# Attention output by features through transfers instead of TensorE transposes

## What is computed

```
q, k, v = split_heads(modulate(ln(x)) @ W_qkv)       # cross: k, v from the context
a = softmax(q @ k.T / sqrt(16))                      # per head
out = (a @ v).reshape(B, tokens, 256)
x = x + gate * (out @ W_out + b_out)
```

## Time and profile before

| | us |
|---|---|
| median of 3 runs (2801.97 to 2818.2) | 2812.86 |
| the profiled execution | 2808.65 |
| its span | 2806.5 |
| TensorE matmul busy | 2694.6 |
| VectorE busy | 1821.8 |
| ScalarE busy | 1442.5 |
| GpSimd busy | 291.4 |

### The profile page before, as it was taken

One profiled execution on the slowest core, in us unless ns is written; L12 is line 12 of the kernel. 1 busy time (PEld: TensorE's weight loads), 2 busy tenths in 40 slices (PEclk: granted clock), 3 DMA queues, 4 the chain that ended last, 5 costly groups with the idle time before them and its releaser, 6 DMA issues.

```text
span 2806.5 us, 57501 instructions
## 1 busy us (share of the span) xinstructions
PE 2694.6 (96%) x21118; PEld 1992.1 (71%) x21118; DVE 1821.8 (65%) x4675; ACT 1442.5 (51%) x2293; POOL 291.4 (10%) x346
## 2 busy tenths in 40 slices
PE   7989999999999999999999999999999999999998
PEld 5656777777776766666777777777776776776777
DVE  4576656755765367675667676676777667676652
ACT  1344554455454556454555555555555555556553
POOL 0000000000001111110111111111000000000000
PEclk9899999999999999998999999999999999999999
DMA  6434243333234365643433333333243332422410
GB/s 201 143 107 126 89 125 103 94 99 128 89 90 126 93 202 168 194 148 105 128 122 116 113 121 109 120 110 121 89 145 111 104 111 87 133 90 81 134 60 17
DMA packets 295964, 326.28 MB, mean 116 GB/s; under 512 B 85386, under 2 KB 186858, under 8 KB 295372
## 3 DMA queue, kind: packets, MB, share of 16 engines
q1 hardware_dynamic: 263244, 275.52, 32.3%
q10 hardware_dynamic: 32256, 47.07, 4.6%
q0 software_dynamic: 192, 0.01, 0.0%
HBM read 203.42 MB, written 118.31 MB: 115 GB/s over the span
## 4 chain that ended last, share of the span: by engine, by line
PE 75%; DVE 11%; DMA 5%; issue 3%; ACT 3%; SPq 2%; POOL 0%; ACTq 0%; DVEq 0%; POOLq 0%
PE gen L1329 12%; PE gen L1320 10%; PE gen L1195 10%; PE gen L1278 9%; PE gen L1161 9%; DVE row_max L1652 6%; PE score L1253 4%; PE score L1208 3%; PE score L1237 3%; PE gen L1289 3%; PE score L1223 3%; PE score L1259 3%; PE gen L1170 2%; PE gen L1300 2%; DMA max_scratch<-maxT 1%
## 5 line engine op out<-in xcount | busy, mean ns | idle before, releaser
L1652 DVE TENSOR_REDUCE row_max<-score 128x4 f32<-128x1024 f32 (+1 forms) x640 | 650.0, 1046 | 123.2 <-PE score L1237 104.4
L1469 ACT ACTIVATE probs<-score 128x1024 f32<-128x1024 f32 (+1 forms) x576 | 567.9, 1023 | 259.6 <-PE score L1253 151.8
L1320 PE MATMUL gen<-xnT,w_w1M 128*128 128x256 f32 x1536 | 361.9, 386 | 1.6 <-ACT xnT L1411 1.6
L1329 PE MATMUL gen<-w_w2M,hT 128*128 128x256 f32 x1536 | 352.3, 383 | 4.5 <-ACT hT L1495 4.4
L1505 POOL TENSOR_TENSOR rstd<-var_eps,minus_half 128x2 f32<-128x2 f32 x160 | 112.0, 700 | 2170.4 <-DVE var_eps L1548 2158.0
L1329 PEld LDWEIGHTS gen<-w_w2M,hT 128*128 128x128 f32 x1536 | 287.0, 191 | 51.5 <-issue 11.8
L1320 PEld LDWEIGHTS gen<-xnT,w_w1M 128*128 128x128 f32 x1536 | 283.7, 191 | 49.4 <-ACT xnT L1411 2.5
L1411 ACT ACTIVATE xnT<-gen,mod_all 128x256 f32<-128x256 f32 x288 | 146.9, 564 | 146.5 <-PE gen L1170 144.3
L1476 ACT COPY oT<-gen 128x512 f32<-128x512 f32 x224 | 131.8, 588 | 163.5 <-PE gen L1278 163.4
L1495 ACT ACTIVATE hT<-gen,b_b 128x256 f32<-128x256 f32 x384 | 157.7, 472 | 112.8 <-PE gen L1320 111.8
L1223 PE MATMUL score<-k_self,q_stack 64*128 64x256 f32 x1536 | 190.4, 340 | 21.3 <-DVE row_max L1652 17.5
(11 more groups left out here) (162 smaller groups left out, 4219.6 us busy)
## 6 DMA issues: line engine op xcount, KB each, us to landing
q_stack<-parts_scratch SPq DMA_DIRECT2D x336, 256.0 KB
parts_scratch<-parts ACTq DMA_DIRECT2D x160, 256.0 KB, 2.6
parts_scratch<-parts SPq DMA_DIRECT2D x160, 256.0 KB, 3.0
k_self<-parts_scratch SPq DMA_DIRECT2D x144, 256.0 KB, 3.7
k_cross<-parts_scratch SPq DMA_DIRECT2D x192, 78.0 KB, 2.5
x_scratch<-x SPq DMA_DIRECT2D x48, 256.0 KB, 3.4
x_in<-x_scratch SPq DMA_DIRECT2D x48, 256.0 KB, 2.8
gate<-gates_scratch SPq DMA_DIRECT2D x80, 128.0 KB, 3.4
```

The source lines that it names most:

```text
L1320: mm = pe.matmul(buf[:, i * S:i * S + S], w["M"]["w1"][:, fc, col:col + P], xnT[s][:, fc, :], start=fc == 0, stop=fc == FC - 1)
L1329: mm = pe.matmul(buf[:, 0:D], hT[:, j, c * P:c * P + P], w["M"]["w2"][:, j, :], start=j == 0, stop=j == FFC - 1)
L1469: act.activation(probs[st.probs][0:keys, :, :], score[st.fill.buf][0:keys, :, :].rearrange("p a (r q) -> p (a r) q", r=2), ACT.Exp, bias=k ...
L1652: dve.tensor_reduce(dst, src, AX_X, ALU.max).then_inc(max_done[b], 1)
```

## The change

The transposes `oX` and `atT` go, and so does `ae`. The stationary operand of `W` is now 32 columns for each head: in `v_self` and `v_cross` two heads lie interleaved (feature d of the one at 1 + 2d, of the other at 2 + 2d, ones at both ends), and the head of a matmul decides at which column its window of 32 starts. So per 32 partitions the heads of the first group have sums in row 0 and features in the odd rows, those of the second group sums in row 31 and features in the even rows; the rows between hold products with the neighbour's columns that nobody reads. `pv` copies the bank to `oT` and the second group also straight into `atT`; then SyncE places the sums of four heads twice (`sg`, two transfers of 4 rows) and the first group's 64 odd rows over the odd rows of `atT` (`sh`). The `oT` buffer comes free when all three have landed. When both halves' sums are there `dv` (`invert`) turns them, takes reciprocals and spreads them over features with a second transpose; `nm` (`divide`) multiplies all of `atT` by them, and `out` may run. The rows of the output weights are loaded in the new order of features by two transfers in place of one. V's copy or bias addition becomes two instructions in place of one.

In the planner, steps of `TRANSFERS` cost 1.4 times their measured time (`MARGIN`), the age of a job counts 16 instead of 12 (`AGE`), and some costs have other values.

```diff
-VC = HD + 1
+VC = 2 * HD + 2
...
+MARGIN, AGE, STAY = 1.4, 16, 4
...
-            "ST": 0.34 + 0.43 * mask if whole else 0.3, "ex": 0.92, "W": 0.99 if whole else 0.56, "pv": 0.48,
-            "oX": 0.44, "dv": 0.63, "atT": 0.22 if whole else 0.44, "ae": 0.26 if whole else 0.48, "out": 1.73,
+            "ST": 0.34 + 0.43 * mask if whole else 0.3, "ex": 0.92, "W": 0.99 if whole else 0.56, "pv": 0.85,
+            "sg": 3.4, "sh": 2.6, "dv": 1.35, "nm": 0.63, "out": 1.73,
...
-        self.before, self.cost = [], cost(blk, name, j)
+        self.before, self.cost = [], cost(blk, name, j) * (MARGIN if name in TRANSFERS else 1.0)
...
-    if name == "oX":
+    if name in ("sg", "sh"):
         gives += ("back",)
...
             pv = add("pv", h, "act", sums, sums[0])
-            oX = add("oX", h, "pe", [pv])
-            divided.append(add("dv", h, "dve", [oX], oX))
...
+            gathered.append(add("sg", h, "sp", [pv]))
+            placed.append(add("sh", h, "sp", [pv]))
+        scaled = add("nm", 0, "dve", [add("dv", 0, "dve", gathered)] + placed)
+        out = add("out", 0, "pe", [scaled])
...
-                st = min(can, key=lambda st: (12 * st.job - st.rank - 4 * (eng == "pe" and TILES.get(st.name, "whole") == self.tiles), 0))
+                st = min(can, key=lambda st: (AGE * st.job - st.rank - STAY * (eng == "pe" and TILES.get(st.name, "whole") == self.tiles), 0))
...
+                def place_sums(st):
+                    s, h, buf = st.slot, st.j, of(st, "pv", st.j).buf
+                    sp.wait_ge(*moved(of(st, "pv", h).fill))
+                    sp.dma_start(sums[s][2 * h + 1:P:VW, 0, :], oT[buf][0:P:VW, 0, :]).then_inc(sums_placed[buf], 16)
+                    sp.dma_start(sums[s][2 * h:P:VW, 0, :], oT[buf][VW - 1:P:VW, 1, :]).then_inc(sums_placed[buf], 16)
+
+                def place_heads(st):
+                    s, h, buf = st.slot, st.j, of(st, "pv", st.j).buf
+                    sp.wait_ge(*moved(of(st, "pv", h).fill))
+                    sp.dma_start(atT[s][1:P:2, h, :], oT[buf][1:P:2, 0, :]).then_inc(heads_placed[buf], 16)
...
-                            mm = pe.matmul(pv[VW * i:VW * i + VC, within, :], value, e, start=kc == 0,
+                            mm = pe.matmul(pv[VW * i:VW * i + VW, within, :], value, e, start=kc == 0,
...
                 def project_out(st):
                     s, blk = st.slot, st.blk
-                    for h in range(HALVES if blk.whole else 1):
-                        pe.wait_ge(*moved(of(st, "atT", h)))
+                    pe.wait_ge(divided, of(st, "nm").nth_all)
...
-                        act.copy(oT[st.buf][:, :, :], pv).then_inc(gen_moved[st.fill.buf], 1)
...
+                        act.copy(oT[st.buf][:, :, :], pv)
+                        act.copy(atT[s][:, j, :], pv[:, 1, :]).then_inc(gen_moved[st.fill.buf], 1)
...
+                def invert(st):
+
+                    s = st.slot
+                    for h in range(HALVES):
+                        dve.wait_ge(*sums_in(of(st, "sg", h)))
+                    link(dve.transpose(sums[s][:, 1, :], sums[s][:, 0, :]))
...
+                    for h in range(HALVES):
+                        dve.wait_ge(*heads_in(of(st, "sh", h)))
+                    dve.tensor_tensor(atT[s][:, :, :], atT[s][:, :, :], inverse[s][:, :, :], ALU.mult).then_inc(divided, 1)
```

More of the change, by code:

```diff
@@ L217, in gives_needed @@
 def gives_needed(blk, ring):
-    return {"hid": TC, "parts": 2, "queries": blk.uses, "gates": TC if blk.kind == "mlp" else 1}.get(ring, 1)
+    return {"hid": TC, "parts": 2, "back": 2, "queries": blk.uses, "gates": TC if blk.kind == "mlp" else 1}.get(ring, 1)
 class Program:
@@ L499, in run @@
                 st.nth_way = seen[st.name, st.slot, "way", st.j, st.blk.whole or st.j == 0]
-def chunks_of(blk, h):
-    return [h] if blk.whole else list(range(FC))
 def column(n):
@@ L839, in dit_stack @@
         xnT = per_slot("xnT", [P, FC, S])
-        at, delta, atT = xhat, xhat, xnT
+        sums, inverse, delta, atT = xhat, xhat, xhat, xnT
         ctx_in = [sb(f"ctx_in{i}", [CTX, D]) for i in range(CTX_IN)]
@@ L869, in dit_stack @@
         rows_ready = [slot_sems(f"rows_ready{h}_") for h in range(HALVES)]
+        sums_placed, heads_placed = ([sem(f"{n}{i}") for i in range(BACKS)] for n in ("sums_placed", "heads_placed"))
+        divided = sem("divided")
         biased = sem("biased")
@@ L1436, in _ @@
                             wait_own(st)
-                            src, out = gen[st.fill.buf][:, :].rearrange("p (c h d) -> p c h d", c=TC, h=H), v_self[own(st)][:, :, :, 0:HD]
+                            src, out = gen[st.fill.buf][:, :], v_self[own(st)][:, :, :, :].rearrange("p c n v -> p (c n) v")
                         else:
                             wait_cross(st)
-                            src, out = gen[st.fill.buf][0:CTX, 0:D].rearrange("p (h d) -> p h d", h=H), v_cross[cross_of(st)][:, :, 0:HD]
-                        act.copy(out, src).then_inc(gen_moved[st.fill.buf], 1)
+                            src, out = gen[st.fill.buf][0:CTX, 0:D], v_cross[cross_of(st)][:, :, :]
+                        for e in range(PER_HALF):
+                            ins = act.copy(interleaved(out, e), by_group(src, e))
+                        ins.then_inc(gen_moved[st.fill.buf], 1)
                     elif st.name == "ph":
@@ L1631, in values @@
                             dve.wait_ge(weighed, before.nth_all)
-                        dve.tensor_tensor(v_cross[cross_of(st)][:, :, 0:HD], src, vb, ALU.add).then_inc(gen_moved[st.fill.buf], 1)
+                        src, vb = gen[st.fill.buf][0:CTX, 0:D], bias_tile(st.blk, "ckv")[0:CTX, :]
+                        for e in range(PER_HALF):
+                            ins = dve.tensor_tensor(interleaved(v_cross[cross_of(st)][:, :, :], e), by_group(src, e), by_group(vb, e), ALU.add)
+                        ins.then_inc(gen_moved[st.fill.buf], 1)
                         return
@@ L1636, in values @@
                         dve.wait_ge(weighed, before.nth_all)
-                    vb = bias_tile(st.blk, "qkv")[:, :].rearrange("p (h d) -> p h d", d=HD)
+                    vb = bias_tile(st.blk, "qkv")[:, :]
                     for c in range(TC):
-                        src = gen[st.fill.buf][:, c * D:c * D + D].rearrange("p (h d) -> p h d", d=HD)
-                        ins = dve.tensor_tensor(v_self[own(st)][:, c, :, 0:HD], src, vb, ALU.add)
+                        src = gen[st.fill.buf][:, c * D:c * D + D]
+                        for e in range(PER_HALF):
+                            ins = dve.tensor_tensor(interleaved(v_self[own(st)][:, c, :, :], e), by_group(src, e), by_group(vb, e), ALU.add)
                     ins.then_inc(gen_moved[st.fill.buf], 1)
```

111 lines of the change are left out of this document (49 added, 62 removed).

## The result

| | before | after |
|---|---|---|
| median, us (range of 7 runs each) | 2812.86 (2801.97 to 2818.2) | 2783.06 (2773.33 to 2796.76) |
| ratio to before, 95% interval | | 0.9904 [0.9883, 0.9926] |
| span of the profiled execution | 2806.5 | 2776.8 |
| TensorE busy | 2694.6 | 2611.1 |
| TensorE idle (span less busy) | 111.9 | 165.7 |

The kernel became about 1% faster where 4.5% was forecast. The range held the time, the likeliest case did not: 30 of the 128 us that it promised came. (Before's range is that of seven runs, not of three.)

The account below looks back on a forecast made before the run. TensorE, busy 96% of the span, was taken as the bound. 2808.65 - 150 (transposes) + 0 (weight loads) + 10 (VectorE) + 12 (SyncE) = 2680.7 us, with 4.2 more against the median 2685 us; range 2615 to 2786.

Parts of the forecast that it names:

- the likeliest case: Whole kernel: the forecast of 2685 us, 4.5% less, with its own range 2640 to 2710; chance 0.63.
- Transposes, -150: TensorE: 1344 transposes go at 0.11 us each, 148 us, with stretches at half clock about 150 us gained.
- the signs named for being right: Among them: W's sixteen matmuls in about 0.99 us, no gap in 500 us of L2, TensorE idle 110 to 140 us.
- Weight loads of W, 0: TensorE: W's loads grow from 17 to 32 columns, 12.5 ns each, hidden; 0, ends 0 and +64 us.
- VectorE, +10: VectorE: 0.82 us more per block, 92 us in all, mostly hidden; +10 us for row maxima waits, ends 0 and +40.
- SyncE, +12: SyncE's queue in L1: six more transfers per block, 38 us added there; +12 us booked, ends 0 and +49.
- the rival, 49: SyncE's queue is the bound in L1: all 49 us instead of 12, 2722 us; chance 0.14.
- ScalarE, 0: ScalarE: copies added and removed make net +19 us on an engine at 51%, hidden by TensorE.
- Latency: From the last W to `out`: 7.2 us, 4.9 more per block, free while TensorE has other sequences.
- The slots: Rival: all six sequences stand in waits at once; 2904 us, or 2858 at half of it; chance 0.07.
- Order, 0 with ends of -20 and +30: All engines: the new instruction order's effect on TensorE's 112 us of idle time, booked as 0.
- the order gives the gain back: Rival: the new order leaves TensorE idle for as long as the transposes took; 2813 us, chance 0.05.

Follow-up runs that it names:

- b_thin: The kernel before, in its own order, with 960 of its 1344 transposes left out and nothing added; 2789.30 us, ratio 0.9896.
- a_neither: The changed kernel in its own order, without the transfers of sums and heads and with the division on VectorE cut to a few columns; 2744.48 us, ratio 0.9740.
- a_no_transfer: The changed kernel in its own order, without the transfers of sums and heads (`sg`, `sh`); 2764.98 us, ratio 0.9823.
- b_order2: The kernel before, planned in another order (transfers at 1.198 times, age 13.34, stay 3.71); 2771.53 us, ratio 0.9871.
- b_age16_m14: The kernel before, planned with age 16 and transfers at 1.4 times their time; 3041.27 us, ratio 1.0821.
- a_dve_small: The changed kernel in its own order, with the VectorE operations of `dv` and `nm` cut to a few columns; 2756.41 us, ratio 0.9774.
- a_age12_m1: The changed kernel, planned with age 12 and transfers at their measured time; 2843.68 us, ratio 1.0124.

## Why the prediction was wrong

**What bounds the kernel: here it failed.** "So time that TensorE gives back is a gain unless another engine or the six slots (the sequences in flight) run out." VectorE at 65% was read as having room. But its work comes in runs: while it does maxima it has none, and in before's order other work, the transposes among it, stood in such places (109.5 to 110.6 us is one). The condition was right and was taken for not met, since it was read from shares over 200 and 500 us and not from what stands between two scores. It was also read from the commonest wait for maxima, 17.5 us, where all such waits are 38.4. b_thin shows it with nothing added: 27% came.

**Transposes, -150: right as a quantity of work, wrong as time.** The rest fell 144 us (131 with idle time at half clock set right); the pitch of the earlier trace rows was the right measure. As time it was worth about half, 73 us, even with both additions gone (a_neither). Of the signs named for being right, idle time of 110 to 140 us and a stretch of 500 us without a gap didn't appear: they are 166 us and 493 of 500.

**A missing term: the clock.** The forecast spoke of "the few stretches at half clock" and booked nothing for more of them. The loss there grew by 60 us (47 without what is idle itself), about as much as the idle time. In L3 one sees what TensorE did before it fell; after, in order of time:

```profile
2115.58 2.00 PE L1191 MATMUL gen<-w_outA,xnT 128*128 128x256 f32 x8
...
2119.84 0.51 PE L1253 MATMUL score<-k_self,q_stack 64*128 64x256 f32 x4 [1.61 <-DVE row_max L1659]
2120.97 0.50 PE L1253 MATMUL score<-k_self,q_stack 64*128 64x256 f32 x4 [0.62 <-DVE row_max L1659]
2122.11 0.50 PE L1253 MATMUL score<-k_self,q_stack 64*128 64x256 f32 x4 [0.63 <-DVE row_max L1659]
2123.24 0.80 PE L1253 MATMUL score<-k_self,q_stack 64*128 64x256 f32 x4 [0.63 <-DVE row_max L1659]
...
2134.56 3.78 PE L1191 MATMUL gen<-maskq,xnT 128*128 128x256 f32 x8
```

Eight scores in a row wait for a row maximum, 1.13 us from one to the next. The first three have 0.5 us of matmuls each; from 2123.24 on the same four take 0.80, and further on, at 2134.56, eight whole matmuls take 3.78 us instead of 2.00. The granted clock is 0.97 from 2119.8 to 2123.2 us and 0.50 from there to 2140. So the clock fell after three gaps of 1.61, 0.62 and 0.63 us and a fourth of 0.63. The Trainium skill ("TensorE: Matmul & The Clock Gate", Part 1) ties the fall of the clock to how busy TensorE has been and names short pauses between groups of matmuls as one cause; this place agrees, with 2.00 us before the pauses and 3.78 behind them.

**Weight loads of W, 0: right.** Loads and matmuls of `W` (count, busy us, mean ns), then sixteen of them in time:

```profile
L1309 PE MATMUL gen<-probs,v_self 128*32 128x256 f32 x3072 | 206.9, 390 | 0.0
...
L1309 PEld LDWEIGHTS gen<-probs,v_self 128*32 128x32 f32 x3072 | 81.9, 110 | 60.4 <-issue 10.7 <-ACT probs L1476 0.6
```

```profile
2114.58 1.07 PE L1309 MATMUL gen<-probs,v_self 128*32 128x256 f32 x16
```

A load takes 110 ns instead of 97, the 13 ns that were estimated, and the next instruction starts at 2115.58, 1.00 us later, where it was 0.99. That holds over the run: where sixteen stand together at full clock the median is 1.001 us (190 times) and was 0.989 (226 times), which makes 4 us over all 5120. The rule of the Trainium skill in "TensorE: Matmul & The Clock Gate", Part 3, that loads overlap only between different groups of rows, would by the prediction's estimate have given 64 us more; the pitch and the fall of the rest by 131 to 144 us leave no room for it.

**VectorE, +10: work right, price likely too low.** The new steps of `dv` and `nm`:

```profile
L1688 DVE STREAM_TRANSPOSE xhat<-row_max 128x512 f32<-128x512 f32 x112 | 79.7, 711 | 3.9
...
L1695 DVE TENSOR_TENSOR xnT<-xnT,xhat 128x512 f32<-128x512 f32 x112 | 76.2, 681 | 20.6 <-DMA xnT<-oT 19.6 <-issue 0.2
...
L1684 DVE STREAM_TRANSPOSE xhat<-xhat 128x256 f32<-128x256 f32 x112 | 47.6, 425 | 12.0 <-DMA xhat<-oT 12.0
L1686 DVE RECIPROCAL row_max<-xhat 128x32 f32<-128x32 f32 x112 | 39.5, 353 | 3.9
```

0.425 + 0.353 + 0.711 + 0.681 = 2.17 us per block, as estimated, and VectorE came to 1914 us (about 1920 forecast). The price of the addition alone wasn't measured: a cut of 157 us of such work brought 37 us (11 either way), so the 92 us that were added cost no more than that. By proportion they cost some 22 us (an estimate), above the 10 booked and within the ends of 0 and 40.

**SyncE, +12: about twice that.** From 1000 to 1200 us it issues 282 times, 162 us by their durations. The forecast had 153, from 115 in before, which by the same count is 119. Yet its queue isn't what TensorE waits for there: its waits are 7.5 us for exponentials, 7.0 for row maxima, 2.8 for `nm` and 0.3 for a transfer. What it costs elsewhere is its order: the placing of sums waits for `pv` (us, times, longest), with all behind it.

```profile
SPq L1092 <- ACT xnT L1486: 186.1, 118, 14.4
```

186 us of standing still look large, but a_no_transfer puts all that the transfers do, this included, at 23 us (8 either way). The price of the rival, 49, didn't come about.

**ScalarE, 0: right.** It has 1423 us, 20 less and not 19 more: there were 102 table loads of its functions instead of 114, and the second copy of `pv` makes 86.

```profile
L1486 ACT COPY xnT<-gen 128x256 f32<-128x256 f32 x224 | 86.3, 385 | 0.0
```

For the wait for `oT` the prediction gave each buffer some 20 us on the mean; its own numbers make 2 x 2806/224 = 25. ScalarE stood 9.8 us in all before `pv` for such a transfer. The waits of TensorE for exponentials, which did grow, don't come from there, since they stay without the transfers.

**Latency.** The heads land in 1.8 us, against the 2.5 taken:

```profile
xnT<-oT SPq DMA_DIRECT2D x224, 64.0 KB, 1.8
```

The slots didn't run out: the one long wait on this path is `out` behind `nm`, 19.2 us in 10 times.

**Order, 0 with ends of -20 and +30: the second step that failed.** By four orders the changed program takes 2754 to 2844 us, by three the old one 2771 to 3041. By ratios that is -28 to +62 around after, and -36 to +231 around before. The ends were too narrow, and a term of 0 can't be kept apart from the others: how much of the transposes' time returns depends on what the order puts in their place. The rival "the order gives the gain back" (0.05) was nearest in its result, but not by its mechanism, since b_thin keeps the order and loses nearly as large a share, 73% against 82.

**What stays open.** Of the 98 us between forecast and result, at most 24 lie in the two additions (46 by a_neither, which cuts more of VectorE's work than was added, less the 22 booked). The other 74 or more are TensorE time that didn't turn into a gain, through gaps and through the clock; how it divides between these two causes can't be told by the runs, because a gap comes ahead of the lower clock. How much of 98 another order takes back is known by three tries: 28 us, 12 us and -62.

## What to carry to other kernels

Where an engine order is fixed and the busiest engine is already interleaved with waits for another, price what is removed from it by its neighbours: look at what stands before each removed instruction and after it, and count it as a gain only where the next instruction doesn't wait for something else. The same length of TensorE time has no one price: transposes spread between other work returned 27 to 37%, a block of them ahead of `out` in the other program cost 80%. Book the clock as a term of its own. Compare two programs only when each has been tried in several orders; here one order alone was worth 36 us and the edit, best order against best, 18.

## What the runs showed of the hardware

The lower clock came without any long pause. In after, at some 2123 us, it followed on steps in which TensorE worked 0.5 of 1.13 us, with the longest gap at 1.61 us: the fourth of them already took 0.80 us for what had taken 0.50, and eight whole matmuls behind them took 3.78 us. Between kernels the loss at half clock and the idle time mostly rise and fall together: 52 us with 74 idle (b_order2), 65 with 112 (before), 125 with 166 (after), 192 with 212 (b_age16_m14). From the least to the most of these, 138 us of idle time go with 140 us more lost to the clock. It is no rule for a single step: a_dve_small idles 20 us less than after and loses 2 more, and a_age12_m1 loses 142 with 202 idle. The loss here counts half of the idle time that lies at half clock too.
